# A decoder layer's recurrence: TensorE's loop written out, three pairs in flight, a new order of work on every engine

## The chip, the core and the metric

One core of a Trainium2 chip runs the whole layer in one launch. The metric is device time in microseconds (us). The engines named here are TensorE (PE: multiplications, with weight loads shown as PEld), VectorE (DVE), ScalarE (ACT), GpSimd (POOL) and SyncE (SP), which issues the DMAs.

## What is computed

The layer has three parts, each with a residual and a layernorm: a gated linear recurrence, a cross attention and a quantized feed-forward. The change lies in the first:

```python
q = (x @ Wq).reshape(b, s, H, HD)          # b = 64, s = 128, D = 256, H = HD = 16
k = (x @ Wk).reshape(b, s, H, HD)
v = (x @ Wv).reshape(b, s, H, HD)
fg = jax.nn.sigmoid(x @ Wf + bf).reshape(b, s, H, HD)
def step(state, inp):
    qt, kt, vt, gt = inp
    state = state * gt[..., None] + vt[..., None] * kt[..., None, :]
    out_t = jnp.einsum('bhij,bhj->bhi', state, qt)
    return (state, out_t)
```

Then come the output's norm, a silu gate and `Wout` (in the second stage's code). All data is float32.

## The kernel before

The stages run one after the other: `recurrence_block`, `attention_block`, `feedforward_block`. In the first, 64 sequences are taken in 32 pairs. The scan over 128 tokens is done as masked products in four chunks of 32 tokens and halves and quarters of the sequence. Gates enter as sums of logarithms: `exponents` multiplies them with 0/1 matrices, five times a pair, and ScalarE takes exponentials of the results (L562).

For one pair the pieces on TensorE are:

- `turn`: four transposes of the input (L347); ScalarE copies them (`turned`, L536) and SyncE stores them for the second stage.
- `value_gate` 0 and 1: values and gates of one sequence, 128 x 512, with a bias product behind (L357, L359). VectorE floors the gate (`floor`, L687); ScalarE copies the values (L544) and makes the gate's logarithm (L545, L548, L550); VectorE splits it in two f16 parts (`split`, L692).
- queries and keys (`across`, L365, four products per half).
- `scores` 0 and 1 (L380, 16 products in 32-row tiles, into four PSUM banks X). VectorE masks each bank (`scores_out`, L678).
- `inside` 0 to 3 (L408, 64 products each, 32x32 tiles, one bank each). VectorE multiplies each by a weight (`inside_out`, L708).
- `across_half` 0 and 1 (L423, 32 products each, 64x64) and `across_quarter` 0 and 1 (L436, 64 products each, 32x32), the work over chunk borders. They reuse banks X0 and X1; VectorE takes them in two and four products (L714).
- VectorE also weights the exponentials by the values (`weighted`, L701, a 2048-wide and a 1024-wide one) and at the end adds six parts to three (`total`, L731); GpSimd adds the three (`gather`, L304 and L306) and SyncE stores the sum.

The order of work is written by hand: each engine has its own program, with semaphores between. All engines hold two pairs, `p` in front (its projections and exponents) and `n = p - 1` behind (scores to borders). TensorE's program is a loop of six steps per turn (`TURNS`, L518), five turns, with the first and last steps outside; VectorE and ScalarE loop over two steps. A float32 product stands once in the program and twice in the trace's counts. GpSimd also rounds the feed-forward weights in 18 pieces between its additions, and VectorE weighs them (`weigh`, L644 to L664) in the first step; after the last pair `weights` transposes and splits weights on all engines.

Of the kernel before, what the change touches and what calls it, by code (L numbers as in the profile page):

```python
# [72 lines left out]
def recurrence_block(nc, t, w, x_d, o_d, xt_d):  # L73
# [24 lines left out]
    TURNS = 6  # L98
    PIECE = FF
    PIECES = 18  # L100
    with ExitStack() as ctx:
# [65 lines left out]
        names = "ident_set w_loaded bf_loaded raw_loaded rest_loaded part all chain weighed rounded turned copied high split cleared".split()  # L167
# [5 lines left out]
        def steps(eng, step):  # L173

            step(0, 0, 0, True, False)
            with eng.Fori(0, (NP - 2) // 2) as j:
                for u in range(2):  # L180
                    step(2 * j + 1 + u, (1 + u) % 2, j + u, True, True)
            step(NP - 1, 1, (NP - 2) // 2, True, True)
            step(NP, 0, NP // 2, False, True)
# [9 lines left out]
        with nc.Block() as block:  # L193

            @block.sync
            def _(sp):
# [24 lines left out]
                for i, name in ((0, "q"), (1, "k")):  # L221
                    sp.dma_start(t["w_rec"][:, :, i, :], w[name].rearrange("(c p) d -> p c d", p=P)).then_inc(qw["w_loaded"], 16)
# [39 lines left out]
            def _(pool):  # L262
# [35 lines left out]
                pool.wait_ge(qw["weighed"], 1)  # L298
# [21 lines left out]
                for flat, r, s in ((flat_u, ru, su), (flat_d, rd, sd)):  # L320
                    for turn_ in range(4):
                        wide = PIECE if turn_ in (0, 3) else 2 * PIECE
                        for at in range(0, flat.shape[1], wide):
                            gather(n, n % 2, n // 2)
                            pool.wait_ge(q["o_taken"], TAKES * (n + 2) + 1)
# [11 lines left out]
            def _(pe):  # L337
# [4 lines left out]
                def turn(p, s, before):  # L342
                    pe.wait_ge(loaded[s], DMAS * (before + 1))
                    wait_if(pe, q["k_ready"], p)
                    for kc in range(KC):
                        for b in range(2):
                            m = T.transpose(F[0][:, (2 * kc + b) * P:(2 * kc + b + 1) * P],  # L347
                                            xs[:, s, b, kc * P:(kc + 1) * P], ident[:])
                    m.then_inc(q["x_made"], 1)

                def value_gate(p, b):
                    if b == 0:
                        wait_if(pe, q["q_ready"], 2 * p)
                    pe.wait_ge(q["xT_ready"], p + 1)
                    bank_ = F[1 - b]
                    for kc in range(KC):
                        T.matmul(bank_[:], xT[:, kc, b * P:(b + 1) * P], wr[:, kc, 2:4].rearrange("p a d -> p (a d)"),  # L357
                                 start=(kc == 0), stop=False)
                    T.matmul(bank_[:, D:], ones_row[:], bf_parts[:], start=False, stop=True).then_inc(q["vf_made"], 1)  # L359

                def across(p, i, bank_, b, oc, done):
                    if oc == 0:
                        pe.wait_ge(q["v_ready"], 2 * p + b + 1)
                    for kc in range(KC):
                        m = T.matmul(bank_[:, oc * 2 * P:(oc + 1) * 2 * P], wr[:, kc, i, oc * P:(oc + 1) * P],  # L365
                                     xT[:, kc], start=(kc == 0), stop=(kc == KC - 1))
                    if oc == KC - 1:
                        m.then_inc(done, 1)

                def scores(n, s, b):  # L370
# [158 lines left out]
            def _(act):  # L529
# [8 lines left out]
                def step(p, s, before, front, back):  # L538
                    if not front:
                        return  # L540
# [1586 lines left out]
```

## Time and profile before

| | us |
|---|---|
| median of three runs | 2018.93 (2016.22 to 2020.7) |
| profiled execution, its own time | 2020.87 |
| its span | 2018.8 |
| mean granted clock of TensorE | 0.972 |

The profile is one execution; a row gives what an engine did, from what start, and in square brackets how long it had been idle before and what released it. "issue" is a wait for nothing that the profile shows. The trace's times are from the span's start. The recurrence takes the first 750 us.

### The profile page before, as it was taken

The numbers are of one execution on the slowest core, as the hardware profiler recorded it, in microseconds if no ns is written. First come the engines' busy times: TensorE is split into PE (matmuls) and PEld (weight loads), VectorE is DVE, ScalarE is ACT, GpSimd is POOL, SyncE is SP. The second block draws the span as 40 slices with busy tenths as digits, with TensorE's granted clock in tenths as the row PEclk, the third lists the DMA queues.
The fourth block names the chain that finished last, engine by engine and source line by source line (L and its number), as shares of the span: only waits on it lengthen the run. The fifth ranks groups of instructions, "written<-read, shape, count | busy, mean of one in ns | idle before, by whom it ended". The sixth has DMA issues, their size and how long they took to land. (4 is left out here: it accounts for less than half of the span.)

```text
span 2018.8 us, 71193 instructions
## 1 busy us (share of the span) xinstructions
PE 1866.0 (92%) x28023; PEld 1301.9 (64%) x28023; DVE 1593.9 (79%) x2870; ACT 1204.5 (60%) x2015; POOL 390.3 (19%) x516
## 2 busy tenths in 40 slices
PE   6999999999999976999999999999599988799798
PEld 4666666666666665888888888887344333344687
DVE  6777777767777774888888888887566799988897
ACT  4444544444545433777777777777355666688465
POOL 1111111211111121233232323232100222100121
PEclk9999999999999988999999999999699999999899
DMA  4111111111111002121212121210288788599574
GB/s 142 39 34 38 47 35 34 38 40 42 34 35 44 30 18 80 47 62 43 62 42 62 42 62 45 59 52 12 47 271 269 275 313 313 185 405 396 184 271 149
DMA packets 169452, 222.03 MB, mean 110 GB/s; under 512 B 80691, under 2 KB 142390, under 8 KB 169270
## 3 DMA queue, kind: packets, MB, share of 16 engines
q1 hardware_dynamic: 169270, 219.22, 32.7%
q8 instruction: 162, 2.65, 0.6%
q14 instruction: 20, 0.16, 0.0%
HBM read 116.40 MB, written 94.37 MB: 104 GB/s over the span
## 5 line engine op out<-in xcount | busy, mean ns | idle before, releaser
L1495 PE MATMUL ff_twin<-ff_xq,w_uh 128*128 (+1 forms) x1152 | 346.6, 383 | 40.3 <-DVE ff_top L1864 25.8
L1495 PEld LDWEIGHTS ff_twin<-ff_xq,w_uh 128*128 128x128 f16 x1152 | 110.6, 98 | 189.5 <-issue 44.2
L1495 PE MATMUL ff_twin<-ff_xq,w_ul 128*128 (+1 forms) x576 | 219.9, 382 | 0.0
L1226 DVE TENSOR_REDUCE mneg<-att_s 128x4 f32<-128x512 f32 x256 | 158.9, 683 | 27.3 <-PE att_s L997 27.2
L562 ACT ACTIVATE x<-rec_e,rec_hidden 128x512 f32<-128x512 f32 x256 | 155.8, 702 | 34.6 <-PE rec_e L396 34.6
L678 DVE TENSOR_TENSOR x<-rec_x,rec_until 128x512 f32<-128x512 f32 x256 | 158.9, 684 | 18.2 <-PE rec_x L380 18.2
L408 PE MATMUL rec_x<-x 32*32 32x64 f32 x8192 | 146.0, 218 | 15.4 <-DVE x L678 11.8
L408 PEld LDWEIGHTS rec_x<-x 32*32 32x32 f32 x8192 | 125.2, 107 | 52.0 <-issue 51.8
L304 POOL TENSOR_TENSOR rec_o<-rec_tmp 128x512 f32<-128x512 f32 x32 | 41.1, 1284 | 575.4 <-DVE rec_tmp L731 575.4
L1143 ACT ACTIVATE att_e<-att_s 128x512 f32<-128x512 f32 x256 | 132.2, 612 | 20.8 <-PE att_s L1030 20.8
L365 PE MATMUL rec_f<-rec_xT,w_rec 128*128 128x256 f32 x512 | 138.5, 405 | 0.0
L357 PE MATMUL rec_f<-w_rec,rec_xT 128*128 128x512 f32 x256 | 129.9, 631 | 6.9 <-DVEq L611 4.8
L714 DVE TENSOR_TENSOR rec_tmp<-rec_x,x 32x256 f32<-32x256 f32 (+1 forms) x192 | 80.8, 421 | 66.8 <-PE rec_x L436 49.6
L708 DVE TENSOR_TENSOR rec_tmp<-rec_x,x 128x512 f32<-128x512 f32 x128 | 84.0, 684 | 57.9 <-PE rec_x L408 57.8
L1925 DVE TENSOR_TENSOR ff_out<-ff_whole,s_other 128x1536 f32<-128x1536 int16 x64 | 112.3, 1760 | 18.4 <-ACT s_other L1682 14.5
L365 PEld LDWEIGHTS rec_f<-rec_xT,w_rec 128*128 128x128 f32 x512 | 91.1, 192 | 32.3 <-issue 10.8
L1929 DVE TENSOR_REDUCE ff_topg<-ff_out 128x1536 f32 (+1 forms) x64 | 110.1, 1743 | 0.2 <-DVE ff_coef L1912 0.2
L562 ACT ACTIVATE x<-rec_e 128x512 f32<-128x512 f32 x64 | 38.1, 597 | 120.1 <-PE rec_e L396 120.1
L701 DVE TENSOR_TENSOR x<-x,rec_v 128x2048 f32<-128x2048 f32 x32 | 73.4, 2293 | 43.9 <-ACT x L562 43.3
L1151 ACT ACTIVATE att_ld<-att_a,part 128x256 f32<-128x256 f32 x128 | 65.2, 560 | 63.5 <-PE att_a L1042 63.1
L1874 DVE TENSOR_REDUCE ff_top<-ff_out 128x1536 f32 (+1 forms) x32 | 56.1, 1754 | 58.3 <-ACT ff_out L1631 58.3
L1495 PEld LDWEIGHTS ff_twin<-ff_xq,w_ul 128*128 128x128 f16 x576 | 56.8, 99 | 67.8 <-issue 2.0
(243 smaller groups left out, 4331.9 us busy)
## 6 DMA issues: line engine op xcount, KB each, us to landing
raw_scratch<-ff_out SPq DMA_DIRECT2D x32, 768.0 KB, 3.5
ff_in<-raw_scratch SPq DMA_DIRECT2D x32, 768.0 KB, 6.1
gate_scratch<-ff_out SPq DMA_DIRECT2D x28, 768.0 KB, 3.6
ff_in<-gate_scratch SPq DMA_DIRECT2D x28, 768.0 KB, 9.6
product_scratch<-ff_out SPq DMA_DIRECT2D x28, 768.0 KB, 9.2
ff_out<-product_scratch SPq DMA_DIRECT2D x28, 768.0 KB, 5.7
turned_scratch<-rec_xT SPq DMA_DIRECT2D x32, 256.0 KB, 3.0
att_x<-in_x SPq DMA_DIRECT2D x32, 256.0 KB, 2.7
```

The source lines that it names most:

```text
L357: T.matmul(bank_[:], xT[:, kc, b * P:(b + 1) * P], wr[:, kc, 2:4].rearrange("p a d -> p (a d)"), start=(kc == 0), stop=False)
L365: m = T.matmul(bank_[:, oc * 2 * P:(oc + 1) * 2 * P], wr[:, kc, i, oc * P:(oc + 1) * P], xT[:, kc], start=(kc == 0), stop=(kc == KC - 1))
L408: m = T.matmul(X[k][rows(c), h * NR * HD:(h + 1) * NR * HD].rearrange("p (r i) -> p r i", r=NR), mt[rows(c), b, hd, rows(c)], e[rows(c), s ...
L562: A.activation(out, E[(s + k) % 2][:], ACT.Exp, bias=hidden[:, asks, r:r + 1] if r < NR else 0.0, scale=-1.0 if asks else 1.0).then_inc(q[ ...
L678: V.tensor_tensor(mt[:, b].rearrange("p (a j m) n -> p j a m n", a=KC, m=2)[:, j], X[j].rearrange("p (a m n) -> p a m n", a=KC, m=2), unti ...
L708: V.tensor_tensor(tmp[:, k * HH:(k + 1) * HH, 0:NR], X[k].rearrange("p (h r i) -> p h r i", r=NR, i=HD), um[:, s, :, k * HH * HD:(k + 1) * ...
L714: V.tensor_tensor(tmp[lanes, b * H:(b + 1) * H, k], bank_[lanes, b * D:(b + 1) * D].rearrange("p (h i) -> p h i", i=HD), e[lanes, s, k, b ...
L1143: A.activation(e[:, b, j], X[j][:], ACT.Exp).then_inc(q["e_ready"], 1)
L1226: V.tensor_reduce(mneg[:, 4 * j:4 * j + 4], X[j].rearrange("p (h k) -> p h k", h=4), AX.X, ALU.max, negate=True).then_inc(q["s_taken"], 1)
L1495: m = T.matmul(bank_.rearrange("p (b n) -> p b n", b=BT), weights(wp, kc, a, c), tile[:, xp, :, kc], start=(i == 0), stop=(i == len(terms) ...
L1925: V.tensor_tensor(ob[:, u, s], whole[:, u, s], other[:, s], ALU.mult).then_inc(q["prod"], 1)
L1929: V.tensor_reduce(topg[:, bass.ds(2 * k + s, 1)], ob[:, u, s], AX.X, ALU.max, apply_absolute_value=True).then_inc(q["maxed"], 1)
```

## The change

Each engine's step now has three pairs: `prev`, `now` and `next_`. The same instructions on data run as before; their order and their waits are other ones.

- TensorE's step is a new list of the pieces, and its 34 steps are written out with no loop, so that waits are on constants.
- ScalarE and VectorE keep loops of two steps, with three steps ahead and behind. ScalarE waits for the constants before its first copy (before: after it).
- The value products come in the order 1, 0; keys and queries are apart; `scores` 0 of a pair is made one step before its `scores` 1.
- VectorE's `total(prev)` stands behind both halves of `scores_out(now)`, ahead of the short `weighted` and of `inside_out(now)`.
- VectorE's `weigh` is cut in three: `weigh_down` and `weigh_up` around the first `split`, the rest after the first pair's `inside_out`. The loads of the q and k weights have a semaphore of their own, and the first products wait for less.
- GpSimd's first `gather` no longer waits for `weighed`; the first rounding does.

The core of the diff (helpers that only take a `Pair` in place of `p, s, before`, and the parts told above, are left out):

```diff
+        class Pair:
...
+            def __init__(self, j, c):
+                self.r, self.s, self.turn = 2 * j + c, c % 2, j + c // 2
+                self.first = isinstance(j, int) and c == 0
+
+        def near(j, u):
+
+            def at(k):
+                if isinstance(j, int) and not 0 <= u + k < NP:
+                    return None
+                return Pair(j, u + k)
+            return at
...
+                def step(at):
+                    prev, now, next_ = at(-1), at(0), at(1)
+                    if prev:
+                        scores(prev, 1)
+                    if now:
+                        exponents(now, 0)
+                        exponents(now, 1)
+                    if prev:
+                        inside(prev, 0)
+                        inside(prev, 1)
+                    if now:
+                        keys(now, 0)
+                    if prev:
+                        inside(prev, 2)
+                    if now:
+                        keys(now, 1)
+                        exponents(now, 2)
+                    if prev:
+                        inside(prev, 3)
+                    if next_:
+                        turn(next_)
+                    if prev:
+                        across_half(prev, 0)
+                    if next_:
+                        value_gate(next_, 1)
+                    if prev:
+                        across_quarter(prev, 0)
+                        across_half(prev, 1)
+                        across_quarter(prev, 1)
+                    if next_:
+                        value_gate(next_, 0)
+                    if now:
+                        scores(now, 0)
+                        exponents(now, 3)
+                        exponents(now, 4)
+                    if next_:
+                        queries(next_)
 
                 pe.wait_ge(qw["ident_set"], 2)
-                turn(0, 0, 0)
-                pe.wait_ge(q["consts_ready"], 1)
-                pe.wait_ge(qw["w_loaded"], 16 * 4)
-                value_gate(0, 0)
-                value_gate(0, 1)
-                products(0, -1, 0, 1, True, False)
-                pieces(0, 0, 0, True, False, True)
-                products(1, 0, 1, 0, True, True)
-                with pe.Fori(0, (NP - 2) // TURNS) as j:
-                    for u in range(TURNS):
-                        p, s = TURNS * j + 1 + u, (1 + u) % 2
-                        pieces(p, s, TURNS // 2 * j + (1 + u) // 2, True, True, True)
-                        products(p + 1, p, 1 - s, s, True, True)
-                pieces(NP - 1, 1, (NP - 2) // 2, True, True, False)
-                products(NP, NP - 1, 0, 1, False, True)
-                pieces(NP, 0, NP // 2, False, True, False)
+                for p in range(-1, NP + 1):
+                    step(near(0, p))
                 weights()
...
+                def step(at):
+                    now, next_ = at(0), at(1)
+                    if now:
+                        exps(now, 0)
+                        queries_out(now)
+                        keys_out(now)
+                        exps(now, 1)
+                    if next_:
+                        turned(next_)
+                    if now:
+                        exps(now, 2)
+                    if next_:
+                        values_out(next_, 1)
+                        values_out(next_, 0)
+                        gate_exp(next_)
+                        gate_log(next_)
+                        gate_high(next_)
+                    if now:
+                        exps(now, 3)
+                        exps(now, 4)
...
+                def step(at):
+                    prev, now, next_ = at(-1), at(0), at(1)
+                    if next_:
+                        floor(next_, 1)
+                    if prev:
+                        half_out(prev)
+                        quarter_out(prev)
+                    if next_:
+                        floor(next_, 0)
+                        if next_.first:
+                            weigh_down()
+                    if now:
+                        scores_out(now, 0)
+                    if next_:
+                        split(next_)
+                        if next_.first:
+                            weigh_up()
+                    if now:
+                        scores_out(now, 1)
+                    if prev:
+                        total(prev)
+                    if now:
+                        weighted(now, 1)
                         for k in range(4):
+                            inside_out(now, k)
+                        if now.first:
+                            weigh()
+                    if next_:
+                        weighted(next_, 0)
+
+                sums()
+                for p in range(-1, 2):
+                    step(near(0, p))
+                with dve.Fori(1, NP // 2 - 1) as j:
+                        step(near(j, u))
+                for p in range(NP - 2, NP + 1):
+                    step(near(0, p))
...
```

TensorE's program of one pair's step before, at the scores; the names are the tiles written and read (`rec_f` the banks of projections, `rec_x` those of scores and results, `x` without a prefix the scratch in `x2` that holds exponentials and masked scores):

```order
L436 MATMUL rec_x<-rec_wa,x 32x16 x32
L357 MATMUL rec_f<-w_rec,rec_xT 128x512 x2
L359 MATMUL rec_f<-rec_bf_parts,rec_ones_row 128x256
L372 ISA
L374 REGISTER_ALU
L380 MATMUL rec_x<-rec_qm,rec_kT 128x256 x8
L363 REGISTER_ALU
L365 MATMUL rec_f<-rec_xT,w_rec 128x256 x4
L376 ISA
L380 MATMUL rec_x<-rec_qm,rec_kT 128x256 x8
```

The same place in the changed program, from the queries of one step into the next:

```order
L387 MATMUL rec_f<-rec_xT,w_rec 128x256 x4
L401 MATMUL rec_x<-rec_qm,rec_kT 128x256 x8
L418 MATMUL rec_e<-rec_nh,rec_sums_of 128x256
L418 MATMUL rec_e<-rec_nlo,rec_sums_of 128x256
...
L430 MATMUL rec_x<-x 32x64 x64
L376 MATMUL rec_f<-rec_xT,w_rec 128x256 x2
L430 MATMUL rec_x<-x 32x64 x32
```

The two halves of the scores (L380 before, L401 now) are no longer a query product apart: half 0 stands ahead of exponents and queries, half 1 begins the next step, and two inside parts (64 in one row) follow two groups of exponents. Further on in the changed step, at the borders:

```order
L445 MATMUL rec_x<-rec_wa,x 64x16 x16
L364 MATMUL rec_f<-w_rec,rec_xT 128x512 x2
L369 MATMUL rec_f<-rec_bf_parts,rec_ones_row 128x256
L459 MATMUL rec_x<-rec_wa,x 32x16 x32
L445 MATMUL rec_x<-rec_wa,x 64x16 x16
L459 MATMUL rec_x<-rec_wa,x 32x16 x32
L364 MATMUL rec_f<-w_rec,rec_xT 128x512 x2
L369 MATMUL rec_f<-rec_bf_parts,rec_ones_row 128x256
L401 MATMUL rec_x<-rec_qm,rec_kT 128x256 x8
```

Quarter, half and quarter parts now follow each other; before, exponents stood between them. VectorE before, one step:

```order
L678 TENSOR_TENSOR x<-rec_x,rec_until 128x2x256 x4
L731 TENSOR_TENSOR rec_tmp<-rec_tmp 128x32x48
L678 TENSOR_TENSOR x<-rec_x,rec_until 128x2x256 x4
L692 TENSOR_TENSOR rec_nlo<-rec_nl,rec_nh 128x512
L701 TENSOR_TENSOR rec_wa<-x,rec_v 128x1024
L708 TENSOR_TENSOR rec_tmp<-rec_x,x 128x8x64 x4
```

and with the change:

```order
L721 TENSOR_TENSOR x<-rec_x,rec_until 128x2x256 x4
L735 TENSOR_TENSOR rec_nlo<-rec_nl,rec_nh 128x512
L721 TENSOR_TENSOR x<-rec_x,rec_until 128x2x256 x4
L771 TENSOR_TENSOR rec_tmp<-rec_tmp 128x32x48
L741 TENSOR_TENSOR rec_wa<-x,rec_v 128x1024
L748 TENSOR_TENSOR rec_tmp<-rec_x,x 128x8x64 x4
```

The split (L692, now L735) moved between the masks, and the sum (L731, now L771) from between them to behind.

## Rows read from the trace of the kernel before

**Rows 1.** The page, busy time of the engines.

```profile
PE 1866.0 (92%) x28023; PEld 1301.9 (64%) x28023; DVE 1593.9 (79%) x2870; ACT 1204.5 (60%) x2015; POOL 390.3 (19%) x516
```

**Rows 2.** Stretch 100:700: us, busy of PE PEld DVE ACT POOL, PEclk, DMA share, GB/s.

```profile
100.00:700.00 600.00, 568.32 (x14131) 399.27 (x14124) 445.75 (x640) 293.01 (x510) 92.57 (x70) 0.99 0.13 37
```

**Rows 3.** Timeline of VectorE, line 731, once per pair: start, us, what.

```profile
147.81 1.75 DVE L731 TENSOR_TENSOR rec_tmp<-rec_tmp 128x1536 f32<-128x1536 f32 x1
169.65 1.75 DVE L731 TENSOR_TENSOR rec_tmp<-rec_tmp 128x1536 f32<-128x1536 f32 x1
195.04 1.75 DVE L731 TENSOR_TENSOR rec_tmp<-rec_tmp 128x1536 f32<-128x1536 f32 x1
...
711.22 1.75 DVE L731 TENSOR_TENSOR rec_tmp<-rec_tmp 128x1536 f32<-128x1536 f32 x1
```

**Rows 4.** Line 518, the loop's jump: ns min/median/max, first and last start.

```profile
L518 PEldq COMPARE_BRANCH  x5: 83/3436/3772, 170.1 to 711.6; - x5
```

**Rows 5.** Waits, 0 to 760 us: us in total, times, longest.

```profile
PEld rec_x L408 <- issue: 51.8, 133, 2.6
```

**Rows 6.** DMA queue of instructions: stretch 174 to 305.8, then 220.5 to 227.7.

```profile
q8 instruction: 26, 0.43, 1.3%
...
q8 instruction: 3, 0.05, 2.7%
```

**Rows 7.** Timeline 400:448, TensorE, part of one step.

```profile
401.85 0.28 PE L396 MATMUL rec_e<-rec_nh,rec_sums_of 128*128 128x256 f16 x1
...
402.39 1.09 PE L408 MATMUL rec_x<-x 32*32 32x64 f32 x64
...
403.42 0.28 PE L396 MATMUL rec_e<-rec_nh,rec_sums_of 128*128 128x256 f16 x1
...
403.86 0.60 PE L347 MATMUL rec_f<-ident,rec_x 128*128 128x128 f32 x4
...
412.23 0.73 PE L436 MATMUL rec_x<-rec_wa,x 32*32 32x16 f32 x64
...
412.88 1.98 PE L357 MATMUL rec_f<-w_rec,rec_xT 128*128 128x512 f32 x4
...
414.85 1.14 PE L380 MATMUL rec_x<-rec_qm,rec_kT 32*128 32x256 f32 x16
...
415.92 1.99 PE L365 MATMUL rec_f<-rec_xT,w_rec 128*128 128x256 f32 x8
...
418.54 1.15 PE L380 MATMUL rec_x<-rec_qm,rec_kT 32*128 32x256 f32 x16 [0.63 <-DVE x L678]
...
419.62 1.13 PE L365 MATMUL rec_f<-rec_xT,w_rec 128*128 128x256 f32 x4
...
420.90 1.09 PE L408 MATMUL rec_x<-x 32*32 32x64 f32 x64 [0.15 <-DVE x L678]
...
421.93 1.13 PE L365 MATMUL rec_f<-rec_xT,w_rec 128*128 128x256 f32 x4
...
422.99 1.10 PE L408 MATMUL rec_x<-x 32*32 32x64 f32 x64
```

**Rows 8.** The same timeline, VectorE and GpSimd.

```profile
413.01 1.77 DVE L714 TENSOR_TENSOR rec_tmp<-rec_x,x 32x256 f32<-32x256 f32 x4 [1.53 <-PE rec_x L436]
...
420.07 2.48 DVE L678 TENSOR_TENSOR x<-rec_x,rec_until 128x512 f32<-128x512 f32 x4
...
420.30 1.28 POOL L304 TENSOR_TENSOR rec_o<-rec_tmp 128x512 f32<-128x512 f32 x1 [15.69 <-DVE rec_tmp L731]
...
421.67 1.27 POOL L306 TENSOR_TENSOR rec_o<-rec_o,rec_tmp 128x512 f32<-128x512 f32 x1
...
422.46 1.02 DVE L692 TENSOR_TENSOR rec_nlo<-rec_nl,rec_nh 128x512 f16<-128x512 f32 x1
...
423.41 1.21 DVE L701 TENSOR_TENSOR rec_wa<-x,rec_v 128x1024 f32<-128x1024 f32 x1
```

**Rows 9.** Timeline 40:43, the split with GpSimd idle.

```profile
41.42 0.68 DVE L692 TENSOR_TENSOR rec_nlo<-rec_nl,rec_nh 128x512 f16<-128x512 f32 x1
```

More of the change, by code:

```diff
@@ L97, in recurrence_block @@
     DMAS = 16 * (1 + NC)
-    TURNS = 6
     PIECE = FF
@@ L166, in recurrence_block @@
         q = {n: sem("rec_" + n) for n in names}
-        names = "ident_set w_loaded bf_loaded raw_loaded rest_loaded part all chain weighed rounded turned copied high split cleared".split()
+        names = "ident_set w_loaded qk_loaded bf_loaded raw_loaded rest_loaded part all chain weighed rounded turned copied high split cleared".split()
         qw = {n: sem("weights_" + n) for n in names}
@@ L556, in step, with keys_out @@
[L556 to L565 removed]
+                def keys_out(p):
+                    act.wait_ge(q["k_made"], p.r + 1)
+                    A.activation(kT[:, p.s].rearrange("p k n -> p (k n)"), F[0][:], ACT.Copy).then_inc(q["k_ready"], 1)
@@ new lines, in exps @@
+                def exps(p, k):
+                    if k == 0:
+                        wait_if(act, q["o_taken"], TAKES * (p.r - 1))
+                    act.wait_ge(q["e_made"], NE * p.r + k + 1)
+                    for asks, r in USES[k]:
+                        out = um[:, p.s, r] if asks else e[:, p.s, r]
+                        A.activation(out, E[(p.s + k) % 2][:], ACT.Exp, bias=hidden[:, asks, r:r + 1] if r < NR else 0.0,
+                                     scale=-1.0 if asks else 1.0).then_inc(q["e_ready"], 1)
@@ L574, in weights @@
                         A.activation(high, W[(WX + i) % len(W)][:], ACT.Copy).then_inc(qw["high"], 1)
-                turned(0)
                 act.wait_ge(q["consts_ready"], 1)
-                steps(act, step)
+                for p in range(-1, 2):
+                    step(near(0, p))
+                with act.Fori(1, NP // 2 - 1) as j:
+                    for u in range(2):
+                        step(near(j, u))
+                for p in range(NP - 2, NP + 1):
+                    step(near(0, p))
                 weights()
@@ L767, in _ @@
+                sums()
+                for p in range(-1, 2):
+                    step(near(0, p))
+                with dve.Fori(1, NP // 2 - 1) as j:
                     for u in range(2):
-                        step(2 * j + 3 + u, (1 + u) % 2, j + 1 + u, True, True)
-                step(NP - 1, 1, (NP - 2) // 2, True, True)
-                step(NP, 0, NP // 2, False, True)
+                        step(near(j, u))
+                for p in range(NP - 2, NP + 1):
+                    step(near(0, p))
```

305 lines of the change are left out of this document (115 added, 190 removed).

## The prediction

> **What bounds the kernel now.** The page comes first. TensorE is busy 92% of the span and VectorE 79% [rows 1], but a share over three stages says nothing of one. The table of stretches gives the recurrence, which ends near 750 us: from 100 to 700 us TensorE is busy 568 of 600 us at a granted clock of 0.99, VectorE 446, ScalarE 293 [rows 2]. A faster order must shorten TensorE's own work or its waits. The change touches no other stage.
>
> The rhythm shows in VectorE's sum of the parts (L731), once per pair of sequences. Most steps last 21.85 us (147.81 to 169.65), yet from 147.81 to 711.22 there are 25 steps in 563.41 us, 22.54 each [rows 3]. So 563.41 - 25 x 21.85 = 17.2 us are lost in a few long steps. The longest, 169.65 to 195.04, has 3.5 us more. TensorE's sequencer stands there at the loop's jump: its compare-and-branch takes 3436 ns at the median [rows 4]. Four returns lie between those rows; their steps, by the same view, are 3.5, some 2, 3.3 and 3.7 us too long, 12.3 us together (what the refilling costs a little later in the step is in it). The remaining 4.9 us, some 6 over the whole recurrence, are issue stalls of 0.3 to 1 us among small tiles (L408 waits 51.8 us for issue in all, most of it in the 0.2 us with which each such group begins) [rows 5].
>
> What a jump has to do with such stalls is in the queue of instruction loads: 26 loads of 16 KB between 174 and 305.8 us, and where small tiles are densest three in 7.2 us [rows 6], so about 3.45 us from one to the next. A step holds some 530 multiplications with a weight load each; 26 loads in six steps makes 4.3 loads a step, 15 us of its 21.85. Loading keeps up on average but not where 256 instructions are used in under 3.45 us.
>
> A step's inside is read from TensorE's timeline, from start to start [rows 7].
> - The exponents' four products take 0.54 us ahead of small tiles (401.85 to 402.39) and 0.44 ahead of wide ones (403.42 to 403.86): turning from wide to small costs 0.1 to 0.2.
> - Four key products take 421.93 to 422.99 = 1.06 ahead of small tiles. Eight take (1.99 - 1.13)/4 = 0.215 each, so the queries started at 415.92 should release TensorE at 417.84; the second half of the scores starts at 418.54, released by VectorE: 0.70 waited. Keys at 419.62 should end at 420.68; the inside work starts at 420.90, again released by VectorE: 0.22 waited.
>
> So 21.85 is 20.9 of TensorE's work and 0.9 of waits for VectorE's masking of scores.
>
> **The change, part by part.**
> 1. *TensorE's order.* All multiplications stay. The first half of the scores and the queries are now made before the step's end, with exponents of the present pair between. VectorE masks half 0 (2.48 us for four, L678 [rows 8]) while TensorE makes exponents 3 and 4 and the queries: 2 x 0.43 + 1.92 = 2.78 us. Its first product follows 0.1 us after the scores, so the mask is ready about when the second half comes: the 0.70 goes. The inside work, which needs half 1, now follows two exponents (0.97 us) and VectorE's first mask: the 0.22 goes. Two of four turns from exponents to small tiles disappear (2 x 0.11) and one from keys (0.21). 21.85 - 0.92 - 0.22 - 0.21 = 20.5 us of TensorE's time per step.
> 2. *What is late next.* The next scores reuse the banks of the border work, which VectorE must have taken. After the second half part TensorE has one quarter part (412.23 to 412.88 = 0.65) and a value product (412.88 to 414.85 = 1.97), 2.62 us, while VectorE has six border products; four take 1.77 us, one every 0.45, so six some 2.65, plus 0.1 until they start and 0.15 until the last is seen [rows 7, 8]. A new wait of 0.28 us is left. Step: 20.5 + 0.28, taken as 20.75.
> 3. *ScalarE and VectorE.* ScalarE's eleven microseconds a step (293/27) have room; its transposed copy is due 0.3 us before the value product that reads it. VectorE has 16.5 us a step (446/27). Its sum (1.75 us) has moved behind both halves of the scores, and GpSimd's two additions (1.28 + 1.27, with their gap 2.64 us from 420.30 to 422.94) [rows 8] now stand between that sum and the first inside product, with only the weighting of 1.21 us beside them. VectorE stands idle for some 1.6 us there. By the order that is free. From the step's start the product ends after scores 1.15, masks 2.40, sum 1.66, additions 2.8 and its own 0.69: 8.7 us. TensorE's border work asks for it after scores 1.07, three groups of exponents and the transposes 2.04, inside 4 x 1.03, keys 1.91: 9.1. This is the least cover of the plan, 0.4 to 0.5 us; behind it queue three inside products, the weighting and the border products, so beyond the 0.5 us it lengthens the step about one for one. The split (L692) leaves GpSimd's company: 1.02 us beside it, 0.68 alone [rows 8, 9], a gain without a taker.
> 4. *The steady part.* 29 such steps: 29 x (21.85 - 20.75) = -32 us.
> 5. *No loop on TensorE.* No jump back: -12.3 us.
> 6. *Loads in straight code.* These stay. From the first inside part to the last quarter part there are 938 instructions, 3.7 loads, in 12.6 us, that is 3.44 us a load: at the limit. Two inside parts now run back to back (256 instructions in 2.06 us), and quarter, half, quarter (320 in 2.35). Walking the written order load by load, each starting when the one before is entered and taking 3.45 us, gives stalls of 0.3 to 1.5 us in two steps of three, 13 us over the recurrence, against the 6 of before: +7 us. Bounds: 0.2 us a step as before (0 us more) and 0.9 us, about the worst stall of before outside the jumps, in every step (+20). I take the walk.
> 7. *Ends.* ScalarE now waits for the constants before its first copy, so the first products start one copy, some 0.6 us, later. VectorE's weighing of the down weights is cut in pieces; the last 2.3 us come after work that TensorE does not await. At the end scores are made a step sooner but the last border work waits as now: -1. Together 0, between -3 and +2.
>
> Sum: -32 - 12.3 + 7 = -37 us. Joints that no row shows (quarter to half part and back, keys and scores to exponents) cost between 0 and the 0.21 of wide to small, four a step: 0 to 24 us; small to wide shows none, so I take 0 and keep 12 for the range. The profiled execution took 2020.87 us with a span of 2018.8; 2020.9 - 37 = 1984. The median of the runs is 1.9 us below it: forecast **1982 us**.
>
> *A rule against item 6.* The rows show stalls at loads in straight code too [rows 5, 6]. The Trainium skill, Runtime: NRT & Kernel Launch, Instruction fetch mechanics, says that crossing a 16 KiB boundary is "mostly hidden" and that a taken branch out of the two-page window forces a fetch before execution goes on. On the branch the trace agrees (3436 ns); on the boundary the 4.9 us disagree. By that rule the written-out program would stall nowhere, and the sum would be -32 - 12.3 - 6 = -50 us.
>
> **The rivals.**
> - *A, as above*, 1970 to 1992 us. 0.72. Its low end is the step without the new wait and with few load stalls.
> - *B, no load stalls at all in straight code:* TensorE's loads never bind once there is no jump. 2018.9 - 50 = 1969 us (by the rows alone: if the stalls of [rows 5] belong to the loop as well). Against it: stalls in the loop's middle, far from any jump. 0.06.
> - *C, the chain sum, GpSimd, inside product becomes the bound.* GpSimd's additions were so far beside VectorE work that reads PSUM [rows 8]; now VectorE's weighting reads two SBUF tiles beside them, and the split shows that company can cost (1.02 against 0.68). If GpSimd is held for the weighting's 1.21 us, the product comes 1.2 - 0.5 = 0.7 us late, +20 us: 2002. For: the small cover. Against: in the rows it is VectorE that loses, never GpSimd. 0.14. The Trainium skill, GPSIMD Engine Reference, Key points, says the two share SBUF interfaces, with contention for VectorE instructions of two SBUF inputs; the split agrees.
> - *D, slower: code loading.* TensorE's dense stretch is already at one load per 3.44 us. Each load that takes d longer costs up to 3.7 d a step: 29 x 3.7 d = 107 d. The gain of 37 is used up at d = 0.35 us if every dense load binds, and by the walk, in which the sparse parts of a step absorb some, at 0.9 us (4.35 us a load). Loads from a program that never comes by twice might be that slow; at 4.5 us a load the walk gives +45 us, 2027 us. Against: the loop's loads are fetched anew in each turn now, at 3.45. 0.04.
> - *E, nothing changes:* some unseen wait holds the step at 21.85 and only the jumps go, but load stalls grow as much. 2018. 0.04.
>
> **How the numbers follow.** A measurement tells 0.2%, 4 us, from no change. Faster: A, B, C, 0.93 with rounding; same: E, 0.03; slower: D, 0.04. The range must leave out no more than 0.2: from 1970 (A's low end, B left out) to 1998, which takes in the 12 us of joints and the nearer part of C.
>
> **What would show it.** The steps of VectorE's sum should be 20.7 to 20.8 us where no load falls badly and 21.1 to 22.2 elsewhere, mean near 21.2. TensorE's compare-and-branch of the recurrence is gone and the loads of code are as many as now. Scores half 1 starts with no wait; scores half 0 waits 0.2 to 0.3 us for a border product. VectorE idles some 1.6 us before the first inside product, released by GpSimd. I am wrong if the undisturbed step is above 21.2 us (joints or C: GpSimd's additions then take longer than 2.7 us or TensorE waits before the first half part), or if the load stalls exceed 20 us (D).

## The result and the profile after

The changed kernel takes **2002.34 us** (median of 4 runs, 1997.83 to 2003.72); the kernel before, run beside it, 2018.18 (4 runs). The ratio is 0.9917, 95% interval [0.9897, 0.9937]: 0.8% faster, 16 us. The forecast was 1982 with a range of 1970 to 1998; the result lies outside, 20 us slow, on the figure that rival C gave. The profiled execution took 2003.72 us, with a span of 2001.6.

The page, and the stretch from 100 to 700 us, as in [rows 1, 2]:

```profile
PE 1860.6 (93%) x28023; PEld 1309.7 (65%) x28023; DVE 1582.8 (79%) x2870; ACT 1197.2 (60%) x2015; POOL 418.0 (21%) x516
```

```profile
100.00:700.00 600.00, 578.77 (x14524) 416.91 (x14526) 450.45 (x663) 295.38 (x525) 116.20 (x70) 0.99 0.13 38
```

TensorE does 14524 multiplications in these 600 us where it did 14131. GpSimd is busy 116 us and was busy 93, though it has only the same additions and pieces of weights to do: something in it takes longer.

The sum, once per pair (now L771; start, us, what), as in [rows 3]. First and 29th, then the two ends of a plain step, then those of the longest step:

```profile
62.55 1.75 DVE L771 TENSOR_TENSOR rec_tmp<-rec_tmp 128x1536 f32<-128x1536 f32 x1
...
674.42 1.75 DVE L771 TENSOR_TENSOR rec_tmp<-rec_tmp 128x1536 f32<-128x1536 f32 x1
...
541.36 1.75 DVE L771 TENSOR_TENSOR rec_tmp<-rec_tmp 128x1536 f32<-128x1536 f32 x1
566.86 1.75 DVE L771 TENSOR_TENSOR rec_tmp<-rec_tmp 128x1536 f32<-128x1536 f32 x1
588.27 1.75 DVE L771 TENSOR_TENSOR rec_tmp<-rec_tmp 128x1536 f32<-128x1536 f32 x1
```

The undisturbed step is 21.42 us (566.86 to 588.27 is one, and 16 of the 28 below lie within 0.02 of it), not 20.75. The 28 steps between the first and the 29th sum take 611.87 us; 28 x 21.42 = 599.8, so 12.1 us are lost beyond that, 9.7 of them in three long steps (the 1st, 12th and 23rd). The same count before (59.48 to 689.37 us) gives 629.89, of which 28 x 21.85 = 611.8 is the plain step and 18.1 the excess. **So of 18.0 us gained in 28 steps 12 are in the plain step and 6 in the excess.** The first sum starts 3.1 us later, for the most part because it now stands behind the masks of both halves; the recurrence ends (the last split of the down weights) at 741.9 where it ended at 757.9; the stages after it take 1.2 us less.

Why the plain step is 21.42, in VectorE's, GpSimd's and TensorE's timelines of one step, as in [rows 7, 8]:

```profile
433.53 1.75 DVE L771 TENSOR_TENSOR rec_tmp<-rec_tmp 128x1536 f32<-128x1536 f32 x1
435.20 1.22 DVE L741 TENSOR_TENSOR rec_wa<-x,rec_v 128x1024 f32<-128x1024 f32 x1
439.00 2.48 DVE L748 TENSOR_TENSOR rec_tmp<-rec_x,x 128x512 f32<-128x512 f32 x4 [2.59 <-POOL rec_o L309]
```

```profile
435.42 2.13 POOL L307 TENSOR_TENSOR rec_o<-rec_tmp 128x512 f32<-128x512 f32 x1 [15.79 <-DVE rec_tmp L771]
437.63 1.27 POOL L309 TENSOR_TENSOR rec_o<-rec_o,rec_tmp 128x512 f32<-128x512 f32 x1
```

```profile
425.61 0.28 PE L369 MATMUL rec_f<-rec_bf_parts,rec_ones_row 3*128 3x256 bf16 x1
425.98 1.34 PE L401 MATMUL rec_x<-rec_qm,rec_kT 32*128 32x256 f32 x16
...
429.97 1.15 PE L401 MATMUL rec_x<-rec_qm,rec_kT 32*128 32x256 f32 x16
...
437.52 1.10 PE L430 MATMUL rec_x<-x 32*32 32x64 f32 x64
438.55 0.66 PE L352 MATMUL rec_f<-ident,rec_x 128*128 128x128 f32 x4
439.80 1.11 PE L445 MATMUL rec_x<-rec_wa,x 64*64 64x16 f32 x32 [0.59 <-issue]
```

Read them from the top. GpSimd's first addition starts 0.22 us after VectorE's weighting has started and takes **2.13 us; it took 1.28** before [rows 8]. The second, which has no company, takes 1.27 as before. VectorE stands for 2.59 us until GpSimd is done and makes the first inside product at 439.00, done at about 439.69. TensorE finished its transposes at 439.1 and has to wait for that product before the first half part: it starts at 439.80, 1.25 us after the transposes began, where without a wait it is 0.59 (below). The wait is put down to "issue", for the semaphore is taken by an instruction of TensorE's queue that is not counted as busy. That it is GpSimd in the end is in VectorE's waits:

```profile
DVE rec_tmp L748 <- POOL rec_o L309: 70.0, 27, 2.6
```

27 of the 32 steps have it.

A second wait is new. The scores at 425.98 write the banks that the border products empty, and VectorE's last six end at 425.83:

```profile
423.15 2.68 DVE L754 TENSOR_TENSOR rec_tmp<-rec_x,x 64x256 f32<-64x256 f32 x6 [0.75 <-PE rec_x L445]
```

The scores start 0.15 us behind that end, and 0.37 us after the product that adds the biases (425.61), where it was 0.05 before (414.80 to 414.85). In 24 of 29 steps between 60 and 700 us the distance to the last border product is 0.14 or 0.15 us. Where TensorE has stopped ahead of them, so that the border products are long done, the scores follow the bias product after 0.00 or 0.01 us. So the 0.37 is the wait for the border products that item 2 of the prediction expects, though the views of waits put it down to "issue".

The longest step, 541.36 to 566.86, in TensorE's timeline, and the granted clock (last column but two) in the stretches around it:

```profile
552.48 0.71 PE L459 MATMUL rec_x<-rec_wa,x 32*32 32x16 f32 x63
554.55 0.18 PE L459 MATMUL rec_x<-rec_wa,x 32*32 32x16 f32 x1 [1.36 <-issue]
554.68 3.77 PE L364 MATMUL rec_f<-w_rec,rec_xT 128*128 128x512 f32 x4
```

```profile
545.00:554.00 9.00, 7.60 (x268) 5.56 (x267) 5.86 (x8) 3.89 (x7) 1.65 (x2) 1.00 0.30 90
554.00:560.80 6.80, 6.25 (x24) 2.68 (x24) 2.40 (x6) 1.51 (x3) 0.00 (x0) 0.50 0.01 4
560.80:570.00 9.20, 8.85 (x236) 6.95 (x234) 8.08 (x11) 5.29 (x10) 1.32 (x1) 1.00 0.01 2
```

TensorE stops 1.36 us between the 63rd and the 64th product of a quarter part, with no operand missing, and for 6.8 us the granted clock is 0.50 (1.2 GHz) before it is 1.00 (2.4 GHz) again. The value product behind the stop takes 3.77 us instead of 1.98. The step is 4.1 us too long: about 1.4 of stop, 1.8 in that product, the rest in the scores. In the DMA records the last load of code ahead of it begins at 552.28 us, 2.3 us before TensorE goes on. From 552.2 to 552.5:

```profile
q8 instruction: 1, 0.02, 18.3%
```

That is no chance: between 60 and 680 us the changed kernel and experiments 3 to 8 have 31 stops of 1 us or more together, and each ends 2.3 to 2.9 us after a load began, though loads are 5.0 us apart in the mean. Two more steps look so (stops of 1.67 us that end at 76.0 and of 1.08 at 315.3, each with 3.4 us of clock 0.5; the steps take 24.56 and 23.86). Behind the 29th sum, outside this count, the clock falls three times more until the recurrence ends, first at 687.

### The profile page after: what moved, and what is told of

Same layout as the page of the kernel before. It is cut to its first block and busy times, and to the rows that moved or that the text cites. A ratio compares the mean times of both kernels' runs of the same rounds, so it can differ in the third digit from the quotient of the medians.

```text
span 2001.6 us, 70719 instructions
## 1 busy us (share of the span) xinstructions
PE 1860.6 (93%) x28023; PEld 1309.7 (65%) x28023; DVE 1582.8 (79%) x2870; ACT 1197.2 (60%) x2015; POOL 418.0 (21%) x516
## 5 line engine op out<-in xcount | busy, mean ns | idle before, releaser
L1535 PE MATMUL ff_twin<-ff_xq,w_ul 128*128 (+1 forms) x576 | 220.5, 383 | 0.0
L307 POOL TENSOR_TENSOR rec_o<-rec_tmp 128x512 f32<-128x512 f32 x32 | 68.2, 2131 | 561.9 <-DVE rec_tmp L771 561.9
L541 ACT ACTIVATE rec_v<-rec_f 128x256 f32<-128x256 f32 x64 | 24.5, 383 | 213.7 <-DVE rec_z L730 213.7
L748 DVE TENSOR_TENSOR rec_tmp<-rec_x,x 128x512 f32<-128x512 f32 x128 | 79.7, 683 | 82.4 <-POOL rec_o L309 70.0
L430 PE MATMUL rec_x<-x 32*32 32x64 f32 x8192 | 139.1, 218 | 4.2 <-issue 3.9
L364 PE MATMUL rec_f<-w_rec,rec_xT 128*128 128x512 f32 x256 | 136.6, 659 | 6.3 <-ACT rec_xT L535 6.3
L1965 DVE TENSOR_TENSOR ff_out<-ff_whole,s_other 128x1536 f32<-128x1536 int16 x64 | 111.8, 1752 | 18.6 <-ACT s_other L1722 14.7
L1820 PE MATMUL ff_twin<-w_dh,s_high 128*128 128x256 f16 x384 | 87.5, 276 | 11.8 <-issue 11.8
L1671 ACT ACTIVATE ff_out<-ff_twin 128x512 f32<-128x512 f32 x96 | 57.2, 596 | 61.8 <-PE ff_twin L1535 61.8
L1430 POOL TENSOR_TENSOR att_ld<-att_ld 128x256 f32<-128x256 f32 x64 | 46.5, 726 | 214.3 <-ACT att_ld L1191 214.3
```

The source lines that it names most:

```text
L430: m = T.matmul(X[k][rows(c), h * NR * HD:(h + 1) * NR * HD].rearrange("p (r i) -> p r i", r=NR), mt[rows(c), b, hd, rows(c)], e[rows(c), p ...
L748: V.tensor_tensor(tmp[:, k * HH:(k + 1) * HH, 0:NR], X[k].rearrange("p (h r i) -> p h r i", r=NR, i=HD), um[:, p.s, :, k * HH * HD:(k + 1) ...
L1535: m = T.matmul(bank_.rearrange("p (b n) -> p b n", b=BT), weights(wp, kc, a, c), tile[:, xp, :, kc], start=(i == 0), stop=(i == len(terms) ...
L1820: m = T.matmul(out, xp[:, u, s, at], t[wp][:, col], start=(s == 0 and xp is hi and b % 2 == 0 and k == 0 and i == 0), stop=(s == 1 and xp ...
L1965: V.tensor_tensor(ob[:, u, s], whole[:, u, s], other[:, s], ALU.mult).then_inc(q["prod"], 1)
```

## The experiments

Every ratio is to the kernel before, run beside it, whose median went from 2017.12 to 2020.54 us between experiments; so a difference between medians of two experiments is not good to less than some 3 us. "Excess" is always what 28 steps, from the first to the 29th sum, take beyond 28 of the plain ones, in the one profiled execution; executions of one kernel differ by up to 14 us, so a difference of a few us between two excesses alone shows nothing.

**1. The old order with TensorE's loop written out** (`e1_unroll`):

```diff
-                with pe.Fori(0, (NP - 2) // TURNS) as j:
+                for j in range((NP - 2) // TURNS):
```

> The old order of work, only TensorE's loop is written out. Theory (jumps cost 12.3 us, loads of instructions still stall straight code at some 3.45 us a load): no compare-and-branch, steps of 21.85 us with some of 22.5 to 23, recurrence 11 to 14 us shorter, about 2005 us. Rival (straight code never stalls): every step 21.85, 18 to 20 us shorter, about 1999 us. Rival (the jump's stall is paid elsewhere): no difference.

Measured: 2012.69 us, ratio 0.9976 [0.9962, 0.9990], 4.8 us less. That is less than the theory's 11 to 14 us. The plain step stays (21.87), no step is over 23.51, the clock does not fall between 60 and 680 us, and the excess goes from 18.1 to 11.0. The loop's returns are gone and about 7 of the 12 us that they cost come back; the rest is lost again in straight code.

**2. The new order with a loop** (`e2_loop`), TensorE's steps in turns of six:

```diff
-                for p in range(-1, NP + 1):
+                for p in range(-1, 1):
+                    step(near(0, p))
+                with pe.Fori(0, (NP - 2) // 6) as j:
+                    for u in range(6):
+                        step(near(3 * j, 1 + u))
+                for p in range(NP - 1, NP + 1):
```

> The changed order of work with TensorE in a loop of six steps again. Theory: the four returns cost what they cost before, some 3 us each, less the long steps that the straight code has at bad places: 6 to 13 us more than the change, 2009 to 2015 us. Rival (the gain of the change is all in the order): 2002 us, as the change.

Measured: 2020.86 us, ratio 1.0017 [1.0005, 1.0029]: 18.5 us over the changed kernel, more than either theory asked; the excess is 33.6. One return, in the timelines of the sum and of TensorE:

```profile
561.41 1.75 DVE L776 TENSOR_TENSOR rec_tmp<-rec_tmp 128x1536 f32<-128x1536 f32 x1
587.78 1.75 DVE L776 TENSOR_TENSOR rec_tmp<-rec_tmp 128x1536 f32<-128x1536 f32 x1
610.99 1.75 DVE L776 TENSOR_TENSOR rec_tmp<-rec_tmp 128x1536 f32<-128x1536 f32 x1
```

```profile
583.48 2.09 PE L401 MATMUL rec_x<-rec_qm,rec_kT 32*128 32x256 f32 x16 [4.10 <-issue]
```

This return makes its step 4.9 us and the next 1.75 us longer (the plain one is 21.46); the others 3.9 to 6.0 and 1.7 to 2.5. TensorE stops for 4.10 us; in the old order its longest stop at a return was 2.2. The clock falls at each of the four returns, where it fell at three of them before. Why a return costs so much more in the new order was not tried. The new order and the written-out program belong together: with the loop it gains nothing at all.

**3. The sum into a tile of its own** (`e3_own`). The first inside product no longer waits for GpSimd; the next sum does, a step later.

```diff
-                        wait_if(dve, q["out_ready"], p.r)
+                        dve.wait_ge(q["w_ready"], 2 * p.r + 2)
...
-                    V.tensor_tensor(tmp[:, :, 0:3], tmp[:, :, 0:3], tmp[:, :, 3:6], ALU.add).then_inc(q["added"], 1)
+                    wait_if(dve, q["out_ready"], p.r)
+                    V.tensor_tensor(three[:], tmp[:, :, 0:3], tmp[:, :, 3:6], ALU.add).then_inc(q["added"], 1)
```

> The change, but VectorE's sum of the parts goes into a tile of its own, so that the first inside product no longer waits for GpSimd's additions. Theory (the chain sum, GpSimd, inside product holds back the border work by 0.66 us a step): undisturbed step 20.76 instead of 21.43, GpSimd's first addition still 2.1 us long, 15 to 20 us less than the change, 1983 to 1988 us. Rival (another wait is as late, such as the border products): step above 21.2, under 6 us gained.

Measured: 1992.86 us, ratio 0.9871 [0.9851, 0.9891], 9.5 us under the changed kernel. Its timelines of VectorE and GpSimd:

```profile
104.38 1.75 DVE L773 TENSOR_TENSOR rec_three<-rec_tmp 128x1536 f32<-128x1536 f32 x1
106.04 1.22 DVE L742 TENSOR_TENSOR rec_wa<-x,rec_v 128x1024 f32<-128x1024 f32 x1
107.36 1.89 DVE L749 TENSOR_TENSOR rec_tmp<-rec_x,x 128x512 f32<-128x512 f32 x3
```

```profile
106.27 2.12 POOL L308 TENSOR_TENSOR rec_o<-rec_three 128x512 f32<-128x512 f32 x1 [16.10 <-DVE rec_three L773]
```

and TensorE's:

```profile
109.40 0.66 PE L353 MATMUL rec_f<-ident,rec_x 128*128 128x128 f32 x4
109.99 1.11 PE L446 MATMUL rec_x<-rec_wa,x 64*64 64x16 f32 x32
```

The addition is as slow (2.12), but nobody waits for it, the half part follows the transposes after 0.59 us, and the plain step is 20.76. That is 28 x 0.66 = 18.5 us off the plain steps. Half of it is given back, so the time is 5 us above the expected range: the excess rises from 12.1 to 21.8, with stops of 1.3 to 1.9 us at six places (a seventh lies behind the 29th sum).

**4. The weighting ahead of the sum** (`e4_weigh_first`), so that GpSimd's additions stand beside nothing:

```diff
+                    if now:
+                        weighted(now, 1)
                     if prev:
                         total(prev)
                     if now:
-                        weighted(now, 1)
```

> The change, but VectorE weights with 1024 columns ahead of its sum instead of behind it, so that GpSimd adds with no SBUF-only VectorE work beside it. Theory (company of the weighting slows GpSimd's first addition from 1.28 to 2.13 us): addition back to 1.28 us, the first inside product some 0.3 us later than in the change, step near 21.75, 2010 us. Rival (the addition is slow for another reason, such as what it reads): addition 2.1 us, step 22.5 or more, 2030 us or more.

Measured: 2007.11 us, ratio 0.9942 [0.9921, 0.9962]. GpSimd's first addition in it, VectorE idle beside it:

```profile
484.82 1.75 DVE L771 TENSOR_TENSOR rec_tmp<-rec_tmp 128x1536 f32<-128x1536 f32 x1
489.38 1.89 DVE L748 TENSOR_TENSOR rec_tmp<-rec_x,x 128x512 f32<-128x512 f32 x3 [2.81 <-POOL rec_o L309]
```

```profile
486.65 1.28 POOL L307 TENSOR_TENSOR rec_o<-rec_tmp 128x512 f32<-128x512 f32 x1 [19.01 <-DVE rec_tmp L771]
```

1.28 us again, in the mean of 30 additions too: the company of the weighting is what costs 0.85. The whole of it stands now ahead of the sum and costs 1.21 on the same chain, so the plain step is 21.70. Both numbers came as expected, and with experiment 3 they settle the mechanism. TensorE's program is that of the changed kernel, and the 1st, 12th and 23rd steps are again the longest (24.67, 25.53 and 24.16).

**5. Every load of code moved by half a load** (`e5_pad`), by increments of a semaphore ahead of the program:

```diff
                 pe.wait_ge(qw["ident_set"], 2)
+                for _ in range(128):
+                    pe.sem_inc(q["seen"], 1)
```

> The changed kernel with 128 semaphore increments ahead of TensorE's program (a few us, and no work with them). They move every later instruction half a load further from where the loads of 256 instructions begin; order, waits and amount of work stay. Theory: the three long steps of the changed kernel (24.6, 23.9 and 25.5 us, eleven steps apart) are those where the begin of a load falls among the quarter, half, quarter parts; so they move to other steps, some three to eight further on, are again about eleven apart, and the time is that of the changed kernel plus or minus 5 us, some 2 us of it the increments. The undisturbed step stays 21.4 us. Rival: the long steps come from the data, the DMA traffic or the chip's clock alone; then they stay at the same three steps.

Measured: 2013.87 us, ratio 0.998 [0.9964, 0.9996], 11.5 us more than without, beyond the 5 expected; the first sum starts 9.8 us later (at 72.38, not 62.55), not 2. The long steps did move by three: they were the 1st, 12th and 23rd, now 25.08, 25.29 and 25.42 us are the 4th, 15th and 26th, still eleven apart. Two of 23.3 came in between. So position in the code decides where they come, not data or DMA traffic alone. The excess of the profiled execution, 22.1, is 10 over that of the changed kernel; it was the slowest of this kernel's ten (2008.98 to 2020.46), so part of that is one execution's luck.

**6. Own tile, and the first quarter part one place earlier** (`e6_own_quarter`), beside experiment 3:

```diff
+                    if prev:
+                        across_quarter(prev, 0)
                     if next_:
                         value_gate(next_, 1)
                     if prev:
-                        across_quarter(prev, 0)
                         across_half(prev, 1)
```

> The kernel whose sum goes to a tile of its own, and in it the first quarter part and its transposes are made one place earlier, so that quarter, half and quarter parts (some 320 instructions of small tiles in 2.35 us) no longer stand back to back. Theory: the stall of 1.3 to 1.9 us at a load of code among them, and with it the fall of TensorE's clock to half that follows for 3 to 7 us, shrink or go; the long steps of 23 to 25 us (four, together some 10 us) fall below 22.5 us, the undisturbed step stays 20.8 us, and the time is 3 to 10 us below that of the kernel with the own tile: 1983 to 1990 us. Rival: the stalls depend on how many instructions are used over a whole stretch, not on these three parts; then the long steps remain, perhaps at other places, and the time is the same within 3 us.

Measured: **1979.22 us**, ratio 0.9817 [0.9799, 0.9835], better than expected and the fastest kernel of the study. The plain step is 20.76, the longest 22.4, the excess 12.3, and from 60 to 680 us the clock is never granted less than full (it falls at 48.5 and from 686.5 on):

```profile
60.00:680.00 620.00, 609.66 (x15575) 442.05 (x15575) 484.44 (x703) 313.53 (x557) 125.36 (x77) 1.00 0.14 39
```

**7. The quarter part alone** (`e7_quarter`), with the sum in its old tile.

> The changed kernel (the sum in its old tile) with the first quarter part one place earlier, and nothing else. The fourth corner of a square with the changed kernel, the own tile, and both. Theory: the two costs are of different kinds and add up. The late first inside product keeps the undisturbed step at 21.4 us; the long steps of 24 to 25 us with a fall of TensorE's clock go. Against the changed kernel that is some 3.1 + 2.4 + 4.1 + 2.3 us of long steps less: 1990 to 1994 us. Rival: most of the 14 us that this move gave beside the own tile came through the wait for GpSimd (a half part that is reached later or earlier); then it gives here under 4 us, over 1998 us.

Measured: 2002.30 us, ratio 0.9901 [0.9877, 0.9925]: nothing against the changed kernel's 0.9917. The theory that the two costs add up fell. The long steps only moved (24.30 and 25.70 for the 5th and 6th, then 23.0 to 23.1 four times), the excess is 18.2 (in this kernel's slowest execution of four, 2009.31 us), and the clock fell six times in 620 us.

**8. Experiment 6 with the increments** (`e8_own_quarter_pad`).

> The kernel with the own tile and the early quarter part, with 128 semaphore increments ahead of TensorE's program, which took some 10 us at the start of the changed kernel and moved every load of code by half a load. Theory: without three border parts back to back no position of the loads is bad, so no step is over 23 us and no fall of the clock stands between 60 and 680 us: 1979 + 10 = 1989 us, plus or minus 3. Rival: the smooth run of the kernel without the increments was a lucky position; then long steps and clock falls return as in the changed kernel with increments (which lost 8 us more than the increments took): 1995 us or more.

Measured: 1998.00 us, ratio 0.9895 [0.9875, 0.9915]. Each theory is half right: no clock fall between 60 and 700 us and a longest step of 23.1, but an excess of 16.3. The median is 18.8 us over experiment 6, and the first sum comes only 8.6 us later. So the quiet run of experiment 6 is in part its position. Without those 8.6 us this kernel would be at 1989.4, only 3.5 under experiment 3; what experiment 3 takes at this position was not tried, so what the early quarter part is worth by itself stays open.

**9 and 10. Small tiles spread further** (`e9_inside_apart`, and `e10_inside_apart_pad` with the increments), beside experiment 6:

```diff
                     if prev:
                         inside(prev, 0)
-                        inside(prev, 1)
                     if now:
                         keys(now, 0)
                     if prev:
+                        inside(prev, 1)
+                    if now:
+                        exponents(now, 2)
+                    if prev:
                         inside(prev, 2)
                     if now:
                         keys(now, 1)
-                        exponents(now, 2)
```

> The kernel with the own tile and the early quarter part; in it the inside products of 64 small tiles alternate with wide work: inside 0, keys 0, inside 1, exponents 2, inside 2, keys 1, inside 3, so that no 256 instructions stand back to back in 2.06 us. Theory: what is lost beyond 28 undisturbed steps (12.3 us there) is stalls at loads of code where small tiles are densest, so it falls to some 5 to 8 us; two more turns from wide to small of 0.1 to 0.2 us a step cost 3 to 5 us. Together the same within 3 us or up to 5 us less than that kernel's 1979 us; the undisturbed step goes from 20.76 to 20.8 to 21.0 us. Rival: the loss is set by how many instructions a step has, not by how they are spread; then it stays at 12 us or more and the time is 3 to 5 us above.

> The same with 128 semaphore increments ahead of TensorE's program, which cost some 9 us at the start and shift the loads of code. Theory: with the small tiles spread the position of the loads matters less, so against the kernel without them it is 9 us longer, plus or minus 3 (the kernel with back-to-back inside parts lost 4 us more than that). Rival: position decides as much as before, and the excess beyond 28 undisturbed steps differs by 4 us or more between the two.

Measured: 1987.27 us (ratio 0.9842 [0.9811, 0.9874]) and 2001.94 (0.9913 [0.9885, 0.9942]). The plain step is 21.00, so the added turns cost 0.24. Between 60 and 680 us no single stop reaches 1 us any more, where experiments 6 and 8 have three and four, yet the excess is 10.7 and 16.5 against their 12.3 and 16.3. Part of it is the clock again: it falls once in experiment 9 and twice in 10, there for 10.2 us in the longest step (25.96). The expected fall to 5 to 8 us was wrong, and so was the 9 us, plus or minus 3, between the two: it is 14.7.

## Why the prediction was wrong

The step that failed is the chain in *ScalarE and VectorE* (item 3). The item took 2.8 us for GpSimd's two additions, "with only the weighting of 1.21 us beside them", and found a cover of 0.4 to 0.5 us. Measured from the second scores (429.97 in this step), TensorE would start the half part 9.17 us later (foreseen: 9.1) and the product is done after 9.72 (foreseen: 8.7). Of the difference 0.85 is the first addition; the rest is in the gaps before and behind the additions (0.22 and 0.10 us, where the working left 0.16 for both). The half part comes 0.66 us late, as rival C had it ("1.2 - 0.5 = 0.7 us late"). Over 28 steps that is 18.5 us, nearly the 20 that the forecast missed. The working had the mechanism, its place and its price, and gave it 0.14 on "in the rows it is VectorE that loses, never GpSimd". In those rows the addition had started first: at 421.67, the split at 422.46 [rows 8], and so in all 30 pairs of that trace. In the changed kernel the weighting starts first in all 31. In both it is the one that starts second that takes longer. The rows had no case with VectorE first, and were read as a rule for who loses.

That one step is not all. With the late product out of the way (experiment 3) the kernel should have taken 1982 us by the working, and took 1992.86. The load term of item 6 was too small at the plain step for which it was worked out: there 28 steps lost 21.8 us and not 18.1 - 5.3 = 12.8. In the changed kernel the term looks right (12.1), but with small moves of the code the excess of written-out orders lies anywhere from 11 to 22, so that is luck.

- *TensorE's order and what is late next* (items 1, 2): 20.75 foreseen, 20.76 measured once the late product is out of the way (experiments 3, 6 and 8). The new wait for the border products was foreseen at 0.28 us; the scores start 0.37 us after the bias product, against 0.00 to 0.05 without a wait, so it is 0.32 to 0.37. This part was right in its mechanism and nearly in its size.
- *The steady part* (item 4): -32 us foreseen; 29 x 0.43 = -12.5 came, 19.5 us less.
- *No loop, loads in straight code* (items 5, 6): -12.3 + 7 = -5.3 foreseen; the excess of 28 steps fell by 6.0. In the old order alone (experiment 1) it fell by 7.1. The four returns of the rows add up to 12.7 rather than 12.3 us. That the sum of the two terms came out is luck, as told above. The walk foresaw stops of 0.3 to 1.5 us in two steps of three and no change of clock; the trace has three long steps, in which the clock costs about as much as the stop. In experiment 3, 17 of 28 steps are 0.3 us or more too long, as the walk had it. The page counts 154 loads of instructions over the whole program, where it was 162.
- *Ends* (item 7): 0 foreseen; +3.1 until the first sum, -1.0 behind the 29th, and -1.2 in the stages behind the recurrence.
- *The rule against item 6.* That crossings are "mostly hidden" (the Trainium skill, Runtime: NRT & Kernel Launch, Instruction fetch mechanics) is not what these traces show: the written-out orders lose 11 to 22 us in 28 steps, with the stops behind loads of code shown above. On the other page of the Trainium skill that was named (GPSIMD Engine Reference, Key points) the traces agree that the two engines disturb each other where VectorE reads two SBUF inputs; it is GpSimd that waits here, 0.85 us of 2.13.
- *Rivals.* B and E are out: code loading did bind, and the time changed. D, over 20 us of load stalls, did not come in the changed kernel; its sign came in experiment 3.
- *The range* had C's nearer part only. With C at 0.14 beside unknown joints, 1998 was too near. That the time fell on C's 2002 is the mechanism and some luck: C took the load term as it stood, and that one fits by luck.

## What to carry to other kernels

Where a plan puts two engines side by side that were not side by side before, price the one that starts second with the whole overlap added, unless a row shows that very pair of operations in that very order; and if the cover is smaller than that, break the dependence (here a tile of 6 KB a partition, since the wait was for a place to write and not for data) ahead of anything else. A written-out program saves only part of what a loop's returns cost, and how much depends on where in the code its loads fall: time two positions before believing a difference of ten microseconds. A shorter step can raise what is lost to loading and to the clock (from 12.1 to 21.8 us in experiment 3), so a gain in the plain step is not yet a gain in time.

## What was not expected of the hardware

- **GpSimd loses most of an overlap with VectorE.** An addition of 128x512 f32 takes 1.28 us alone or beside operations that read PSUM, and 2.13 beside a product of two SBUF inputs (128x1024 f32, 1.22 us) that began 0.22 us earlier: of 1.00 us side by side 0.85 are lost. The product takes no longer than in company of nothing (1.21). In the kernel before it was the other way about: there the addition began first and the split paid, 1.02 for 0.68 [rows 8, 9].
- **A stop of TensorE and its clock.** In the changed kernel each of the three falls of the granted clock to 0.5 between 60 and 680 us begins within 0.6 us of the end of a stop of 1.1 to 1.7 us, and they last 3.4 or 6.8 us. It is no rule: experiment 8 has four stops of 1.2 to 1.9 us with the clock at full, and experiment 10 falls twice, for 3.4 and 10.2 us, without a stop of 1 us. What decides it stays open; experiments 6 and 8, with a plain step of 20.76 and the early quarter part, had none between 60 and 680 us, and neither had experiment 1.
- **128 increments of a semaphore on TensorE take some 19.5 us**, 0.15 us each. They start at 1.58 us, and TensorE's first transposes start at 21.10 where they started at 4.64. Only 8.2 to 9.8 of that reach the first sum, since TensorE waits 4.64 us for its input and 5.37 us for ScalarE's copy without them. From experiment 5:

```profile
21.10 1.09 PE L352 MATMUL rec_f<-ident,rec_x 128*128 128x128 f32 x4 [21.10 <-issue]
```

What stays open besides: why the excess does not shrink when small tiles are spread. It is 10.7 to 12.3 us in two orders at one position and 16.3 to 16.5 at the other, so in these four it goes with the position and not with the order, but each is one execution, and executions of experiment 10 alone differ by 14 us. Whether another position is better than both was not tried.
